# Six PSUM banks between score products and shifted products: from three and three to two and four, in both attentions of a decoder layer

## The reference: what is computed

```python
scores = jnp.einsum('bhqd,bhkd->bhqk', q, k) * scale    # self: masked above the diagonal
attn = jax.nn.softmax(scores, axis=-1)
out = jnp.einsum('bhqk,bhkd->bhqd', attn, v)
# cross: K and V from ctx_1024 (2048 keys), no mask
```

## Time and profile before

| | |
|---|---|
| median of 3 runs | 4606.11 us (4603.25 to 4610.75) |
| profiled execution | 4606.11 us, of it span 4604.4 us |
| TensorE busy | 4057.2 us (88%) |
| VectorE busy | 2742.5 us (60%) |
| GpSimd busy | 2478.5 us (54%) |
| ScalarE busy | 2095.8 us (46%) |
| self loop | 394.7 to 1072.9 us |
| cross loop | 1815.4 to 3587.9 us |

### The profile page before, as it was taken

How to read it: one execution, slowest core, us unless ns; L and a number is a source line. 1 busy time by engine, 2 the same in 40 slices (tenths; PEclk the granted TensorE clock), 3 DMA queues, 4 the chain that set the end, 5 groups by cost and what they waited for, 6 DMA issues and landing times. The chain is left out here.

```text
span 4604.4 us, 61752 instructions
## 1 busy us (share of the span) xinstructions
PE 4057.2 (88%) x21906; PEld 2506.8 (54%) x21906; DVE 2742.5 (60%) x4978; ACT 2095.8 (46%) x3869; POOL 2478.5 (54%) x927
## 2 busy tenths in 40 slices
PE   6998999997779998999999999999999653439997
PEld 5874555555568885444444444444444432328886
DVE  4436777772443336777777777777775332216665
ACT  2113555553121111666666666666666222216665
POOL 0001333331000002999999999999999224528887
PEclk9997999998889997999999999999999865569998
DMA  4546344314555555222222222222220465524444
GB/s 147 173 164 144 87 105 110 87 40 148 186 187 172 172 169 135 54 56 58 56 56 56 56 56 56 56 56 56 56 56 6 162 182 100 84 61 74 82 80 64
DMA packets 283654, 449.72 MB, mean 98 GB/s; under 512 B 31960, under 2 KB 132312, under 8 KB 277208
## 3 DMA queue, kind: packets, MB, share of 16 engines
q1 hardware_dynamic: 259640, 407.27, 33.9%
q0 software_dynamic: 19776, 36.85, 4.7%
q10 hardware_dynamic: 3968, 2.10, 0.2%
HBM read 267.22 MB, written 178.91 MB: 97 GB/s over the span
## 5 line engine op out<-in xcount | busy, mean ns | idle before, releaser
L665 POOL TENSOR_TENSOR cross_partial<-cross_partial,cross_probs 128x2048 f32<-128x2048 f32 x320 | 1465.7, 4580 | 66.5 <-ACT cross_probs L832 29.4
L881 DVE TENSOR_REDUCE cross_neg_max<-cross_scores 128x1 f32<-128x512 f32 x2048 | 1265.7, 677 | 395.2 <-PE cross_scores L708 395.1
L832 ACT ACTIVATE cross_probs<-cross_shifted 128x512 f32<-128x512 f32 x2048 | 1074.5, 606 | 743.3 <-PE cross_shifted L720 709.2
L708 PE MATMUL cross_scores<-cross_k_stack,cross_q_stack 96*128 96x512 f32 x2048 | 875.9, 437 | 39.4 <-DVE cross_neg_max L881 27.4
L720 PE MATMUL cross_shifted<-cross_q_stack,cross_k_stack 98*128 98x512 f32 x2048 | 850.6, 420 | 13.8 <-DMA cross_q_stack<-cross_neg_dram 5.8
L720 PEld LDWEIGHTS cross_shifted<-cross_q_stack,cross_k_stack 98*128 98x128 f32 x2048 | 387.2, 190 | 385.4 <-issue 236.4
L708 PEld LDWEIGHTS cross_scores<-cross_k_stack,cross_q_stack 96*128 96x128 f32 x2048 | 395.0, 193 | 287.2 <-DVE cross_neg_max L881 224.6
L832 ACT ACTIVATE self_probs<-self_shifted 128x512 f32<-128x512 f32 (+3 forms) x768 | 358.6, 492 | 367.1 <-PE self_shifted L723 286.2
L881 DVE TENSOR_REDUCE self_neg_max<-self_scores 128x1 f32<-128x512 f32 (+3 forms) x768 | 388.4, 548 | 208.1 <-PE self_scores L708 108.2
L736 PE MATMUL cross_out<-cross_probs,cross_v 128*32 128x512 f32 x4096 | 494.1, 600 | 0.0
L708 PE MATMUL self_scores<-self_k_stack,self_q_stack 96*128 96x512 f32 (+3 forms) x768 | 308.2, 422 | 23.6 <-DMA self_k_stack<-k_hi 10.0
(11 more groups left out here) (249 smaller groups left out, 6294.6 us busy)
## 6 DMA issues: line engine op xcount, KB each, us to landing
cross_k_stack<-k_hi SPq DMA_DIRECT2D x30, 1024.0 KB, 20.1
out_a_in<-attn SPq DMA_DIRECT2D x16, 1024.0 KB, 9.7
x<-out_y SPq DMA_DIRECT2D x16, 1024.0 KB, 5.3
kv_x_in<-in_ctx SPq DMA_DIRECT2D x16, 1024.0 KB, 5.4
k_hi<-kv_out_hi SPq DMA_DIRECT2D x64, 256.0 KB, 2.6
k_lo<-kv_out_lo SPq DMA_DIRECT2D x64, 256.0 KB, 3.2
v<-kv_out_n SPq DMA_DIRECT2D x64, 256.0 KB, 2.3
cross_v<-v SPq DMA_DIRECT2D x32, 512.0 KB, 25.1
```

The source lines that it names most:

```text
L665: nc.gpsimd.tensor_tensor(total, total, own, ALU.add).then_inc(pool_added.sem, 1)
L708: mm = nc.tensor.matmul(scores[at][:, 0:width], q_st[0:96, w, h, q0:q0 + P], k_st[0:96, w, h, half * WIDE:half * WIDE + width], start=True ...
L832: nc.scalar.activation(probs[:, e % NE % PB, h, f:], shifted[n % SHIFTED][:, f:], ACT.Exp).then_inc(exped.sem, 1)
L881: nc.vector.tensor_reduce(neg_max[:, q % 2, column(a), half:half + 1], scores[n % (SLOTS * ROUNDS) % AHEAD][:, 0:width], AX.X, ALU.max, ne ...
```

## The change

Of the six banks, four instead of three take shifted products and two instead of three take scores. Nothing else is edited; the waits above follow from the two constants.

```diff
@@ -400,8 +400,8 @@
     SETS = keys // P
     WIDE = 512
     HALVES = keys // WIDE
-    SHIFTED = 3
-    AHEAD = 3
+    SHIFTED = 4
+    AHEAD = 2
     PER_GROUP = 1 if causal else 2
     BUFS = 4 // PER_GROUP
     ROUNDS = 4
```

## The result

The changed kernel takes 4889.76 us (median of 4 runs, 4886.64 to 4892.49) against 4608.43 us, a ratio of 1.0613 with a 95% interval of 1.0599 to 1.0626: 281 us slower, where 275 was forecast. The total is nearly right by luck: two terms were wrong in opposite directions, and the stretches show which. The profiled execution has a span of 4890.8 us.

A forecast was written before the change was run, and what follows sets the result against it. TensorE was taken as the bound, its score banks already short. From 4606.11 us, the terms 210 + 13 + 53 + 3 - 4 = +275 us gave 4881 us, with a range from 4805 to 4930 us.

The forecast's parts named there:

- What bounds the kernel: TensorE, about 98% busy in both attention loops; score banks already short, with cross-loop waits for VectorE of 200.6 and 27.4 us.
- Cross, the price of a cycle: Cross loop: with two score banks a one-burst cycle's last score slips from 3.56 to 4.36 us, costing 0.80 us.
- half cycle: Cross loop, half of a cycle with a second burst (sums): 0.47 us more each, 0.94 per cycle.
- The rule of two banks: Score n waits for reduce n-2's end; 0.54 + 0.68 + 0.07 = 1.29 us for two scores, 0.645 each.
- rival 1: VectorE stays fed, its 0.60 us decides in cross, self costs only its low bound: 4835 us, chance 0.15.
- Cross, the sum: Cross loop: 2.40 + 1.35 + 2.82 = 6.6 us a block, times 32 blocks: +210 us (184 to 225).
- The shifted side: Fourth shifted bank saves under 0.6 us at each of some ten pass wraps: -4 us (0 to -11).
- Opening: Before the first shifted product, scores slow down: cross +13 us (0 to 16), self +3 us (0 to 7).
- Self: Self loop: wide score pieces stall, also behind reciprocals, about 3.3 us for each of 16 rounds: +53 us (25 to 70).
- rival 2: TensorE's clock falls; with a tenth of the cross loop at half clock, 160 us more, 5040 us; chance 0.06.
- my own list: Signs of a wrong prediction: scores staying 0.60 us apart, the clock dropping, or the self loop growing by another size.
- Rivals 3 and 4: ScalarE was the hidden limit, 4470 us, chance 0.02; no change because both effects are small, 4606 us, chance 0.02.

The follow-up runs named there:

- shift3_score2: Three shifted banks kept, two score banks instead of three, one bank empty, against the kernel before the change: 4889.82 us (ratio 1.0653).
- lead18_33: Three and three banks, score products in cross 18 instead of 16 slots ahead, against the kernel before the change: 4596.84 us (ratio 1.0010).
- shift2_score4: Two shifted and four score banks instead of three and three, against the kernel before the change: 4671.26 us (ratio 1.0176).
- half_33: Three and three banks, each row maximum over the first half of its piece's columns, against the kernel before the change: 4501.26 us (ratio 0.9800).

## Why the prediction was right

- **What bounds the kernel.** Right: `shift3_score2` has the whole loss with the shifted side untouched, and the score waits went from 228 to 541 us.
- **Cross, the price of a cycle.** The places of the scores in the changed kernel are right to 0.01 us in the plain cycle and the half cycle, and to 0.05 with reciprocals. The rule of two banks with 0.54 + 0.68 + 0.07 is what the trace shows, and rival 1 (VectorE stays fed at 0.60) is out by the 0.645 of the reduces. The loop's total alone would not have told: +185 is by chance what rival 1's low bound (+184) says.
- **Cross, the sum.** Mis-sized twice. A block grew by 6.2 us where I had 6.6. By the start times of the bursts, averaged over the blocks, the six half cycles with a second burst cost 2.86 us (2.82 forecast), but the five other cycles 3.37 and not 3.75. Why they cost less than the cycle worked stays open; taking away the wait for the maxima's transfer did not settle it (`lead18_33`). And I multiplied by 32 blocks. From the second turn to the last, 30 blocks, the time went from 1671.5 to 1858.3 us, +187. Ahead of the second turn the loop grew by 5. In the last block there are no scores, so nothing to lose, and the fourth shifted bank makes it 6.3 us shorter. That is the +185, to a microsecond. I knew from the code that scores run a block ahead; the multiplication should have been by 31 less a gain.
- **The shifted side.** I gave it -4 us for wraps. The wraps gave 1.4 us in cross (7 x 0.2); the larger gains, 6.4 and 3.4 us, lie in the last stretch of each attention, where I hadn't looked: about -11 in all by the traces.
- **Opening.** +13 and +3 forecast, +12.3 and +3.6 measured: in cross the way from the first score to the turn grew by 12.9 us (40.8 to 53.7) at a clock of 0.50, and the rest, which holds the DRAM trip, did not grow.
- **Self.** The mechanism was right, the size too small twice, and +84 lies above the bound of 70. My terms for a round, 1.66, 1.7 and 0.3, add up to 3.7 us; the sum went on with 3.3. Measured are 4.6 without the clock. One round with its turns and three of its bursts, before and changed (TensorE's timeline; the clock is at 1.00 in both):
```profile
685.54 0.29 PE L696 MATMUL self_scores<-ident,self_neg 128*128 128x128 f32 x1
686.89 1.92 PE L736 MATMUL self_out<-self_probs,self_v 128*32 128x512 f32 x16
...
714.48 0.86 PE L736 MATMUL self_out<-self_probs,self_v 128*32 128x256 f32 x16
...
721.84 1.92 PE L736 MATMUL self_out<-self_probs,self_v 128*32 128x512 f32 x16
728.46 0.33 PE L696 MATMUL self_scores<-ident,self_neg 128*128 128x128 f32 x1
...
926.31 0.28 PE L696 MATMUL self_scores<-ident,self_neg 128*128 128x128 f32 x1
928.53 1.92 PE L736 MATMUL self_out<-self_probs,self_v 128*32 128x512 f32 x16
...
957.52 0.86 PE L736 MATMUL self_out<-self_probs,self_v 128*32 128x256 f32 x16
...
966.33 1.92 PE L736 MATMUL self_out<-self_probs,self_v 128*32 128x512 f32 x16
973.93 0.28 PE L696 MATMUL self_scores<-ident,self_neg 128*128 128x128 f32 x1
```
  The heavy stretch around the turn costs 0.98 us ahead of it and 0.87 behind it, 1.85 (1.66 worked); the heavy steps before it, from 714.48 to 721.84, 1.45 (1.7 worked). The rest of the round, which I put at 0.3, costs 1.40 (27.59 to 28.99): there lies the error of the waits. The other 20 us come from rival 2, the falling clock, which I had placed in the cross loop at a chance of 0.06. There it stayed at 1.00. In self it fell behind the turn between two reciprocals, for about 7 us in the round shown (a mean of 0.93 over 50.2 us). By my own list a falling clock and another size of self were signs that the prediction is wrong, and both came; the score waits, the spacing and the block came as listed.
  The Trainium skill (TensorE: Matmul & The Clock Gate, "A second HAM failure mode: psum-queue depth-cycling") says that small gaps from cycling through PSUM banks can make the clock swing; the falls in the self loop agree with it as far as two banks bring them, but each stands behind a turn and they go with the reciprocals, so it is not the cycling alone. The cross loop at 1.00 does not show it, though its score waits are five times as long in total (541 us against 80.2 + 25.6 in self).
- **Rivals 3 and 4.** Out: nothing was hidden, and `shift2_score4` shows that neither side had a bank to spare.

The errors, -21 in the cross loop and +31 in self, mostly cancelled, and the total came out 9 us above the 4881 forecast; a reader should trust the cycle and not the total.

## What to carry to other kernels

A ring of n banks between two engines can be free only while n times the producer's spacing exceeds the hold (product to reader, the reader's full latency, the way back): here 3 x 0.467 = 1.40 us against 0.43 + 0.68 + 0.07 = 1.18, and with two banks 0.93 against it. The reader's own pace, 0.60 a reduce, is a second bound. Work the hold out with the latency of a stalled product (0.54), and count each other instruction of the reader's queue as hold: in self the 0.94 us reciprocals cost waits and clock with two banks. Work every part of a round and not only the heavy one. Count blocks by the loop that issues the waiting instruction, and look at the last block by itself: what is short there can be another ring.

In these runs shortening the hold pays more than moving banks: with half maxima and three and three banks the kernel takes 4501 us, 2% less than before and faster than both kernels of this case. Softmax is the same function whatever number is subtracted, but a row's largest score may then lie above the subtracted one, so the guard against overflow is weaker; whether that is acceptable depends on the data.

## What the runs showed of the hardware that I had not expected

- The clock of TensorE fell to its lower level and came back in nine of the 14 full rounds of a self loop in which TensorE is busy 95% of the time (726.28 of 762.10 us), while it stayed at 1.00 in a cross loop with 97% (1896.82 of 1957.90 us). So the busy share and the total of the waits did not tell where it falls; the place did, 0.4 to 1.8 us behind the turn. Shorter reciprocals on another engine, 0.94 us each before, stopped it. Half maxima left one fall.
- A single longer gap was followed by a fall too: in `half_33`, whose cross loop is otherwise at 1.00 up to its last turn, TensorE idles 2.02 us up to 2214.35, and from 2214.50 to 2217.90 the clock is 0.50. Five more gaps of 1.8 to 2.3 us, one in four blocks, each have such a fall behind them.
